# First cross attention: in even rounds SyncE moves the rows of maxima before it loads the next head's keys

## The reference, cut to what matters

```python
x = x + _L0_xattn_ref(_layernorm(x), ctx_2048)

q = qkv.reshape(bs * 16, 16, 512)          # 16 heads of 16 channels
k = v = y.reshape(bs * 16, 16, 8192)       # keys = values, 8192 of them a head
weight = softmax(einsum('bct,bcs->bts', q * scale, k * scale), axis=-1)
a = einsum('bts,bcs->bct', weight, v)
```

## Time and profile before

| what | value |
|---|---|
| median of 3 runs | 1379.47 us (1379.35 to 1380.12) |
| profiled execution, its own time | 1378.92 us |
| its span in the trace | 1377.1 us |
| PE, DVE, ACT, POOL busy | 97%, 80%, 70%, 11% of the span |
| first cross attention | from the start to about 665 us |
| distance of one round start from the next | about 19 us |

### The profile page before, as it was taken

How to read it: one execution, slowest core, us unless ns; L and a number is a source line. 1 busy time by engine, 2 the same in 40 slices (tenths; PEclk the granted TensorE clock), 3 DMA queues, 4 the chain that set the end, 5 groups by cost and what they waited for, 6 DMA issues and landing times. The chain is left out here.

```text
span 1377.1 us, 28335 instructions
## 1 busy us (share of the span) xinstructions
PE 1337.2 (97%) x10623; PEld 883.4 (64%) x10623; DVE 1098.5 (80%) x2195; ACT 970.5 (70%) x1892; POOL 156.2 (11%) x216
## 2 busy tenths in 40 slices
PE   3999999999999999999999999999999999999999
PEld 3544444444444444444458999999988874668998
DVE  5899999998999999997877666666668759887665
ACT  1499999998999999999574555555544631785553
POOL 4122222122222222112000000000000000000000
PEclk9899999999999999999999999999999999999999
DMA  7665556655666555565204755555529614204651
GB/s 190 123 144 126 118 140 161 154 144 131 149 159 132 130 133 130 125 92 79 100 1 151 298 186 187 185 186 188 190 91 370 244 69 177 69 1 131 181 190 39
DMA packets 75914, 199.51 MB, mean 145 GB/s; under 512 B 35576, under 2 KB 43680, under 8 KB 64128
## 3 DMA queue, kind: packets, MB, share of 16 engines
q1 hardware_dynamic: 75600, 197.69, 50.9%
q10 hardware_dynamic: 192, 0.20, 0.1%
HBM read 170.64 MB, written 23.80 MB: 141 GB/s over the span
## 5 line engine op out<-in xcount | busy, mean ns | idle before, releaser
L754 ACT ACTIVATE probs<-bank 128x512 f32<-128x512 f32 x1024 | 541.8, 620 | 51.4 <-PE bank L812 49.1
L672 DVE TENSOR_REDUCE pm<-bank 128x1 f32<-128x512 f32 x736 | 466.4, 682 | 49.3 <-PE bank L793 48.8
L812 PE MATMUL bank<-qst,kst 52*128 52x512 f32 (+1 forms) x1024 | 336.3, 437 | 6.1 <-DMA qst<-nscratch 5.8
L793 PE MATMUL bank<-kst,qst 48*128 48x512 f32 x904 | 315.2, 451 | 21.5 <-DMA qst<-qsplit 20.5
L824 PE MATMUL bank<-probs,vext 128*32 128x256 f32 (+3 forms) x4024 | 294.9, 394 | 0.7
L812 PEld LDWEIGHTS bank<-qst,kst 52*128 52x128 f32 (+1 forms) x1024 | 163.8, 187 | 195.0 <-DVE pm L672 93.8
L1602 PE MATMUL bank<-e_xhi,e_hi 128*128 128x256 f32 (+1 forms) x768 | 217.4, 283 | 0.3 <-DVE e_xlo L283 0.2
L1602 PE MATMUL bank<-e_xhi,e_lo 128*128 128x256 f32 (+1 forms) x768 | 217.3, 283 | 0.0
L1602 PE MATMUL bank<-e_xlo,e_hi 128*128 128x256 f32 (+1 forms) x768 | 217.2, 283 | 0.0
L824 PEld LDWEIGHTS bank<-probs,vext 128*32 128x32 f32 x4024 | 92.3, 109 | 117.2 <-issue 103.4
L793 PEld LDWEIGHTS bank<-kst,qst 48*128 48x128 f32 x904 | 140.6, 189 | 31.2 <-DMA qst<-qsplit 20.5
(11 more groups left out here) (251 smaller groups left out, 1764.9 us busy)
## 6 DMA issues: line engine op xcount, KB each, us to landing
raw<-wall SPq DMA_DIRECT2D x43, 1536.0 KB, 6.5
kst<-kscratch SPq DMA_DIRECT2D x192, 128.0 KB, 4.5
kscratch<-ksplit SPq DMA_DIRECT2D x15, 1024.0 KB, 4.4
kraw<-ctx_rows SPq DMA_DIRECT2D x16, 512.0 KB, 6.0
vraw<-ctx_vt SPq DMA_DIRECT2D x16, 512.0 KB, 6.1
ctxT<-ctxT SPq DMA_DIRECT2D x8, 1024.0 KB, 9.7
nat<-ctx_chunks SPq DMA_DIRECT2D x6, 1024.0 KB, 19.0
weights<-wscratch SPq DMA_DIRECT2D x16, 256.0 KB, 5.6
```

The costliest lines, as they stand in the source:

```text
L672: nc.vector.tensor_reduce(max_at(p, 1), bank[:, pre_bank(p), :], AX.X, ALU.max).then_inc(pre_reduced, 1)
L754: nc.scalar.activation(probs[:, (XST * k + n) % PR, :], bank[:, score_bank(XST * k + n), :], ACT.Exp, scale=XSCALE).then_inc(probs_ready, 1)
L793: ins = nc.tensor.matmul(bank[:, pre_bank(p), :], qst[64 * j:64 * j + KR, h, tt * P:tt * P + P], keys, start=True, stop=True)
L812: nc.tensor.matmul(bank[:, score_bank(s), :], kst[64 * j:64 * j + rows, h % 2, m * P:m * P + P], qst[64 * j:64 * j + rows, h, :], start=Tr ...
```

## The change

`load_stack(h + 1, 0)` moves behind `stack_negmax(NS * h)` in SP's program, for h = 0 to 14. `spread_weight(h - 1)` keeps its place ahead of `stack_negmax`, so that it is now directly behind the loads of the queries. Nothing is added or taken away, and no other engine's program changes.

```diff
@@ -503,8 +503,6 @@
                             row = 64 * j + KR
                             sp.dma_start(kst[row:row + 4, b, :].bitcast(F32),
                                          marks[:, :, :].rearrange("k s n -> k (s n)").bitcast(F32)).then_inc(negmax_stacked, 16)
-                if h < XH - 1:
-                    load_stack(h + 1, 0)
                 if h == XH - 1:
                     sp.wait_ge(o_stored[1], 16 * (XH // 2 - 1))
                     for n in range(XHA + 3, XH - 2):
@@ -513,6 +511,7 @@
                     spread_weight(h - 1)
                 stack_negmax(NS * h)
                 if h < XH - 1:
+                    load_stack(h + 1, 0)
                     load_apart(h + 1, 0)
                 if h == 0:
                     load_raw(2)
```

## The result

The changed kernel is slower: 1386.29 us (median of 6 runs, 1382.45 to 1392.89) against 1379.41 us for the kernel before on the same chip; ratio 1.0055, 95% interval 1.0034 to 1.0075. The forecast was 1373.4, its own range 1371.5 to 1376, and up to 1379.0 where the gain is taken back in part; what happened is the fourth rival, priced at 1385.5. The profiled execution is the slowest of the six: 1392.89 us, its span 1391.1. What it loses against the profile of before, 14.0 us of span, is twice what the medians show; the places are to be read from it, the size from the medians.

The account below looks back on a forecast made before the run. PE, busy 97% of the span, bounds the kernel; time returns only where it stands still or clocks lower. Even rounds 5.1, odd writes -0.5, round 0 1.5 make 6.1 us: 1379.47 to 1373.4, range 1371.5 to 1376.

Parts of the forecast that it names:

- the gain is taken back in part: Rival: odd rounds of heavy passes wait 0.3 to 0.5 us each, round 0 gives nothing; 1378.4 us, chance 0.15.
- the fourth rival: Odd write in heavy passes held by 768 KB of keys; PE waits 1.4 us in nine rounds; 1385.5 us, chance 0.16.
- The even rounds: Even rounds h >= 1: write of the maxima meets an empty queue, 1.42 us instead of 4.83; gain 5.1 us.
- The later keys: Key loads behind the even write end at +9.2 us, wanted at +16.7; no wait of `pre` for keys.
- what is late next: the write of the odd round: Odd write behind the larger backlog: SP resumes at +22.7 us, +23.5 allowed; cost 0.5 us, bounds 0 and some 8.
- The 0.8 us of room: Heavy passes, odd write: margin between SP resuming at +22.7 us and the +23.5 allowed before PE waits; called thin.
- the slow side: Slower outcome: odd writes of heavy passes held by the moved keys, 1385.5 us or up to 1398; chance 0.16.
- The price behind a wait: Lower clock after a PE wait: 1.4 us behind a wait of 1.70, none behind waits of 0.76.
- Round 0: Start of the stage: the 2.62 us wait goes and the clock stays up; gain 1.5 us, bounds 3.5 and 0.
- the new wait at round 1: Round 1's write held by the largest backlog, through at 64.7 to 65.2; PE waits 1.3 us, 0.7 charged for clock.

Follow-up runs that it names:

- e5: The change in passes 0 to 13, next-stage loads ahead of the even write in passes 3 to 10, against the kernel before: 1376.44 us, ratio 0.9996.
- e4: The change in passes 0 to 13, with raw rows, pairs and next-stage loads ahead of the even write, against the kernel before: 1374.32 us, ratio 0.9974.
- e11: As e5, with two more dummy matmuls behind each of the first two items of round 0, against the kernel before: 1374.95 us, ratio 0.9973.

## Why the prediction was wrong, by its own steps

- **The even rounds** went as reckoned in kind: no wait is left in any, and in the light passes the write resumes after 1.4 to 2.3 us. In passes 3 to 10 it takes 1.6 to 3.0, not 1.42, with the DMA engines almost idle (pass 4: 2.74). I did not find out why.
- **The later keys** never held PE up; no wait of `pre` for `kst` appears.
- **The step that failed** is "what is late next: the write of the odd round". I reckoned that SP resumes at +22.7 us from the even write, against +23.5 allowed. In pass 4 it resumed at 227.01 - 201.32 = +25.7; 2.2 beyond the allowed, and PE waited 2.00. The mechanism was named, the sizes were too small, all to one side: the keys start moving about 1.1 later, because the even write took 2.74; the half-0 keys need 6.0 (half of the 12.0 us above), not 5.1, because I shared out a window of keys and broadcast by bytes, and key bytes are the slower ones; the rest of the backlog 0.6 more; and SP comes back 2.3 us after its end, not 1.85. Together 3.0. The end of the backlog, at 224.75 - 201.32 = +23.4 against +20.8, is well read; how its 2.6 us are shared between the start, the keys and the rest is an estimate, good to some 0.3 us.
- **The 0.8 us of room** was smaller than the sum of these errors, and I gave the slow side 0.16 on it, with 0.5 us as the cost. Eight rounds crossed the line together: the odd rounds of passes 3 to 9, which have the same backlog, and round 29; round 21, with the same backlog too, just missed it (4.55 us). Had I set the keys at their own rate, the room would have been gone before any other error (6.0 for 5.1 is 0.9, against 0.8).
- **The price behind a wait** was put at 1.4 us at most. Behind 2.00 us it was 4.1 (round 9: 23.03 less 18.95), behind 2.44 it was 2.8 (round 7: 208.53 - 186.81, less 18.95), and behind 1.94 (round 29) nothing.
- **The fourth rival's mechanism** is the one that came; that its 1385.5 lies so near is in part luck. It reckoned nine waits of 1.4 us and nothing behind them; the trace has eight of 1.5 on average and 8.7 us behind them, in the slowest execution.
- **Round 0** gave 1.6 us against 1.5 forecast, by another way, so the agreement is luck: the clock did fall there, and the new wait at round 1 did not come, because that backlog was through at about 63, when the write went out (62.98; SP resumed at 65.25), and not at 64.7 or later. DVE's pairs stopped PE for 0.54 and 0.63 us ahead of the fall; e5 has the same two stops and no fall, so why it fell is open.

## What to carry to other kernels

When a small latency-bound transfer shares the DMA engines with bulk, moving bulk from one side of it to the other moves the hold to the next small transfer: write down, for both, the time at which all bytes in front have passed, with each kind of load at its own measured rate. A room that is smaller than the error of that sum is no room, above all where many equal rounds would cross the line together. Shifting the fast loads the other way, into the hole that the keys left, brought the medians of both writes under their limit and took the loss away. The fastest kernels run, e4 and e11, are 0.26 and 0.27% faster than before; how much of that is from these loads and how much from round 0 (pass 0 alone has 0.15%, and e11 has the dummies) is not told apart, and single writes of both still go over the limit (4.92 us in round 8 of e4, 5.39 in round 14 of e11).

## What the runs showed of the hardware that was not expected

- A write on GpSimd's queue is held by SP's bulk in flight nearly as one on SP's is: 4.73 us against 2.06 in quiet, on SP's queue 4.83 against 1.42.
- The same write took 1.4 us in some passes and 1.6 to 3.0 in others with the DMA engines almost idle; no run shows why.
- The key loads, onto 16 partitions each, fill all DMA engines at 138 GB/s, the loads behind them, mostly onto 128, at 357. Their shapes differ in more than the partitions; which part sets the rate was not tried.
- The granted clock fell in round 0 of the changed kernel with PE stopped for only 0.54 and 0.63 us between single matmuls, and did not in e5, where PE runs the same program and has the same stops. In the steady rounds it stayed at 1.00 behind stops of 0.96, 1.03 and 1.94 us (rounds 11, 13 and 29) and fell behind 1.77, 2.00 and 2.44 (rounds 15, 9 and 7; 0.81, 0.57 and 0.63 over the 9 to 11 us behind). The length of the stop alone does not decide it.
